# Cross attention of a perceiver: five of seven value units move into their own batch's steps, the opening block is reordered, the context comes in pieces

## The chip, the core and the metric

The program runs on one core of one Trainium2 chip. The metric is the device time of one execution in microseconds (us). TensorE is called PE, VectorE DVE, ScalarE ACT, GpSimd POOL; SP is the engine that here only issues DMA transfers.

## What is computed

Two layers of a perceiver are computed. Each layer has a cross attention over a context, a self attention and a feed-forward part. Only the first part, the cross attention of layer 0, is touched here:

```python
x, ctx_1024            # (16, 64, 256) and (16, 1601, 256), float32
# 16 heads of 16; q from layernorm(x), k and v from the context of the same batch
q = layernorm(x) @ wq + bq
k = ctx_1024 @ wk + bk          # 16 x 1601 x 256
v = ctx_1024 @ wv + bv
p = softmax(q @ k.T * 16 ** -0.5)     # per head
x = x + (p @ v) @ wo + bo
```

The key and value projection of layer 1's cross attention (one shared head of 16) reads the same context and is computed here too ("shared" below), and stored in DRAM for later.

## The kernel before

`cross_attention_block` does the 16 batches one after the other. The work of one batch has two kinds.

**Projection units.** The context of a batch (1602.0 KB, `ctx[b % 2]`, two buffers) is turned into keys and values in 17 units, each a few matmuls of PE into one bank (`project`, L675) and one eviction by DVE (`move_projection`, L702): eight units of keys (two groups of heads, four stretches of columns each), one "shared", seven of values (two tiles of 128 keys each, the last 65 rows), and "turn", which transposes what "shared" gave. POOL splits each unit of keys into a high and a low part (`split_keys`, L643), and counts it in the semaphore `keys_split`.

**Attention steps.** Eight steps n = 0 to 7 for a batch, a pair of heads each. A step has two halves of scores (`score`), two reductions on DVE (`maximum`), two exponentials on ACT (`exps`), and the transposes of the exponentials of the step before (`turn`). Four steps are a group, and `weigh` multiplies a group's probabilities by the values: group 0 of a batch in step 5, group 1 in step 1 of the next batch.

PE runs both kinds in one hand-written order: in each step of batch b it does scores, one unit of batch b+1, transposes, scores, another unit of batch b+1, transposes. Even slots hold keys, odd slots hold "shared" and then the seven values; slot 16 is "turn". The last batch has no units in its steps. Batch 0 has its 17 units in an opening block (`first_block`), which also normalises x, projects the queries (four units, two PSUM banks), stores them in DRAM and loads them back as `q_stack`.

**SP's queue.** SP copies the split keys of batch b+1 into the operand of the scores, `k_stack[n]`, as soon as step n of batch b has been scored, four transfers of 200.2 KB for each n (`stack_keys`). It runs in a fixed order, in which each wait holds back all that stands behind it:

```python
for n in range(PAIRS):
    if n % GROUP_PAIRS == 0:
        sp.wait_ge(keys_split, K_UNITS * (b + 1) + CHUNKS_PER_GROUP * (n // GROUP_PAIRS + 1))
    sp.wait_ge(scored, 2 * (PAIRS * b + n + 1))
    stack_keys(sp, n)
```

At n = 0 it waits for the first four units of keys of batch b+1 (slots 0, 2, 4, 6), and at n = 4 for all eight; the eighth stands in slot 14, in step 7. After n = 7 come the load of the queries of batch b+2, then the context load of batch b+3 (once all units of batch b+1, which read the same buffer, are done), then a store. PE waits for a context at slot 0 (`ctx_loaded` in `project`), just behind the first half of scores of step 0.

A block ends with a barrier of all engines: the next one starts when each engine, SP among them, has come to its end.

Of the kernel before, what the change touches and what calls it, by code (L numbers as in the profile page):

```python
# [21 lines left out]
TILES = TOKENS // P  # L22
# [542 lines left out]
def cross_attention_block(core, layer, x, wo, wk, wv, bk, bv, bo, w_shared, b_shared, scratch, heads_t):  # L565
# [13 lines left out]
    assert U == 2 * PAIRS + 1  # L579

    with ExitStack() as stack:
# [36 lines left out]
        def load_q(sp, b, parity):  # L618
            for copy in range(COPIES):
# [19 lines left out]
        def store_values(sp, b, parity):  # L639
            sp.wait_ge(projection_moved, U * (b + 1))  # L640
            sp.dma_start(core.v1_scratch[b], v_shared[parity][:].rearrange("p t d -> p (t d)")).then_inc(values_stored[parity], 16)

        def split_keys(pool, b, u):  # L643
            g, s, w = k_units[u]
            pool.wait_ge(projection_moved, U * b + units.index(("keys", u)) + 1)
# [8 lines left out]
        def split_shared(pool, b):  # L654
            pool.wait_ge(projection_moved, U * b + units.index(("shared", 0)) + 1)
# [7 lines left out]
        def split_parts(pool, b):  # L663
            for what, i in units:
# [5 lines left out]
        def project(pe, b, parity, u, bank, moved):  # L670

            if u == 0:
                pe.wait_ge(ctx_loaded[parity], 8 * (b - parity) + 16)
            if moved > 0:
                pe.wait_ge(projection_moved, moved)  # L675
            what, n = units[u]
# [25 lines left out]
        def move_projection(dve, b, parity, u, bank):  # L702
            dve.wait_ge(projection_done, U * b + u + 1)
            what, n = units[u]
# [31 lines left out]
        def first_block(first):  # L736
# [11 lines left out]
            EARLY = 3  # L748
# [3 lines left out]
            keys_loaded = core.sem(first, f"{layer}_keys_loaded")  # L752
            values_loaded = core.sem(first, f"{layer}_values_loaded")
# [17 lines left out]
            with core.block() as block:  # L771
                @block.sync
                def _(sp):
                    for i in range(HALVES):
                        half = slice(i * TILES // 2, (i + 1) * TILES // 2)
                        sp.dma_start(x[:, half], dram["x"][:, half]).then_inc(x_loaded[i], 16)
                    sp.dma_start(core.ident[:], dram["ident"]).then_inc(ident_loaded, 16)
                    sp.dma_start(wk[:], dram[f"{layer}_wk"]).then_inc(keys_loaded, 16)
                    sp.dma_start(bk[:], dram[f"{layer}_bk"]).then_inc(keys_loaded, 16)
                    sp.dma_start(w_shared[:], dram["L1_xattn_wkv"]).then_inc(keys_loaded, 16)  # L780
                    sp.dma_start(b_shared[:], dram["L1_xattn_bkv"]).then_inc(keys_loaded, 16)
                    load_ctx(sp, 0, 0)
                    sp.dma_start(wq[:], dram[f"{layer}_wq"]).then_inc(query_loaded, 16)
                    sp.dma_start(bq[:], dram[f"{layer}_bq"]).then_inc(query_loaded, 16)
                    sp.dma_start(wv[:], dram[f"{layer}_wv"]).then_inc(values_loaded, 16)
# [11 lines left out]
                    load_q(sp, 0, 0)  # L797
# [14 lines left out]
                def _(pe):  # L812
                    pe.wait_ge(ident_loaded, 16)
# [8 lines left out]

                    def project_first(u):
                        if u == 0:
                            pe.wait_ge(keys_loaded, 16 * 4)
                            pe.wait_ge(bank_ready, 1)
                        if units[u] == ("values", 0):
                            pe.wait_ge(values_loaded, 16)
                        project(pe, 0, 0, u, banks[:, u % 4], max(u - 3, 0) if units[u][0] != "turn" else u)

                    for u in range(EARLY):
                        project_first(u)
                    pe.wait_ge(query_loaded, 32)
                    for i, (m, half) in enumerate(q_units):
                        pe.wait_ge(x_turned_moved, half + 1)
# [6 lines left out]
                        project_first(EARLY + i)  # L842
# [2206 lines left out]
```

## Time and profile before

| | |
|---|---|
| median of three runs | 2355.4 us (2355.22 to 2358.36) |
| the profiled execution | 2351.33 us, span 2349.1 us |
| PE | busy 92% of the span |
| DVE, ACT, POOL | busy 56%, 42%, 14% |
| granted TensorE clock, mean | 0.959 of full speed |
| context loads (`L_xattn_ctx`) | 16, 1602.0 KB each |

The first attention takes some 890 us of the span. Clocks are shares of TensorE's full speed: 1.0 is its level of 2.4 GHz, 0.5 that of 1.2 GHz. A DMA's time to landing is from its issue to its semaphore.

### The profile page before, as it was taken

The numbers are of one execution on the slowest core, as the hardware profiler recorded it, in microseconds if no ns is written. First come the engines' busy times: TensorE is split into PE (matmuls) and PEld (weight loads), VectorE is DVE, ScalarE is ACT, GpSimd is POOL, SyncE is SP. The second block draws the span as 40 slices with busy tenths as digits, with TensorE's granted clock in tenths as the row PEclk, the third lists the DMA queues.
The fourth block names the chain that finished last, engine by engine and source line by source line (L and its number), as shares of the span: only waits on it lengthen the run. The fifth ranks groups of instructions, "written<-read, shape, count | busy, mean of one in ns | idle before, by whom it ended". The sixth has DMA issues, their size and how long they took to land. (4 is left out here: it accounts for less than half of the span.)

```text
span 2349.1 us, 39843 instructions
## 1 busy us (share of the span) xinstructions
PE 2168.8 (92%) x15922; PEld 1499.2 (64%) x15922; DVE 1315.5 (56%) x2292; ACT 997.3 (42%) x1868; POOL 331.6 (14%) x366
## 2 busy tenths in 40 slices
PE   7999999999999977999998899978999999887796
PEld 4777777777777754555554677854555554545795
DVE  4566666656665634555553344447777772667554
ACT  1555555555555552333433011114666665516121
POOL 3322222232222200000000000014000000000241
PEclk9999999999999978999999899998999999898798
DMA  6877776777777521000000212113111111013312
GB/s 200 197 171 183 179 174 154 173 178 171 183 178 176 127 59 51 6 12 6 6 1 1 115 68 94 55 45 78 28 33 36 24 24 31 23 43 136 135 48 78
DMA packets 101338, 216.18 MB, mean 92 GB/s; under 512 B 58738, under 2 KB 66299, under 8 KB 95428
## 3 DMA queue, kind: packets, MB, share of 16 engines
q1 hardware_dynamic: 98420, 204.93, 35.3%
q0 software_dynamic: 2208, 6.03, 0.8%
q10 hardware_dynamic: 528, 2.69, 0.4%
q8 instruction: 127, 2.08, 0.4%
q14 instruction: 55, 0.45, 0.1%
HBM read 91.16 MB, written 15.20 MB: 45 GB/s over the span
## 5 line engine op out<-in xcount | busy, mean ns | idle before, releaser
L1089 DVE TENSOR_REDUCE L_xattn_maxima<-L_xattn_scores 128x1 f32<-128x1024 f32 (+1 forms) x256 | 253.6, 991 | 239.4 <-PE L_xattn_scores L1012 239.0
L1156 ACT ACTIVATE L_xattn_probs_t<-L_xattn_turned 128x1024 f32<-128x1024 f32 (+1 forms) x256 | 220.8, 862 | 332.6 <-PE L_xattn_turned L1024 332.6
L1997 DVE TENSOR_REDUCE shared_half_maxima<-shared_ring 128x1 f32<-128x578 f32 (+1 forms) x251 | 244.4, 991 | 89.9 <-PE shared_ring L1903 87.1
L2077 ACT ACTIVATE shared_exps<-shared_scores 128x512 f32<-128x512 f32 (+1 forms) x416 | 225.7, 594 | 122.6 <-PE shared_scores L1924 122.0
L1168 ACT ACTIVATE L_xattn_probs<-L_xattn_scores,L_xattn_maxima 128x1024 f32<-128x1024 f32 (+1 forms) x256 | 235.6, 925 | 37.7 <-DVE L_xattn_maxima L1092 37.7
L1024 PEld LDWEIGHTS L_xattn_turned<-ident,L_xattn_probs 128*128 128x128 f32 x1664 | 197.3, 144 | 79.7 <-issue 46.7
L1024 PE MATMUL L_xattn_turned<-ident,L_xattn_probs 128*128 128x128 f32 x1664 | 233.9, 280 | 12.9 <-ACT L_xattn_probs_t L1156 12.0
L686 PE MATMUL L_xattn_projected<-L_xattn_wv,L_xattn_ctx 128*128 128x256 f32 x780 | 193.0, 389 | 0.0
L680 PE MATMUL L_xattn_projected<-L_xattn_ctx,L_xattn_wk 128*128 128x400 f32 x480 | 182.0, 501 | 0.0
L1012 PE MATMUL L_xattn_scores<-L_xattn_k_stack,L_xattn_q_stack 128*128 128x512 f32 (+1 forms) x512 | 159.0, 392 | 22.2 <-ACT L_xattn_probs L1168 11.0
L1924 PE MATMUL shared_scores<-shared_q,shared_k 128*128 128x512 f32 (+1 forms) x416 | 154.1, 449 | 0.1
L686 PEld LDWEIGHTS L_xattn_projected<-L_xattn_wv,L_xattn_ctx 128*128 128x128 f32 x780 | 136.7, 186 | 21.3 <-issue 0.5
L1903 PE MATMUL shared_ring<-shared_k,shared_q 128*128 128x512 f32 x502 | 134.4, 366 | 12.9 <-DMA shared_q<-q_scratch 7.4
L649 POOL CAST L_xattn_k_part<-L_xattn_k_part 128x400 fp32r<-128x400 f32 (+1 forms) x128 | 66.5, 519 | 549.5 <-DVE L_xattn_k_part L710 549.5
L1442 ACT ACTIVATE wide_probs<-wide_scores,wide_stats 128x1024 f32<-128x1024 f32 x64 | 71.4, 1115 | 153.9 <-DVE wide_stats L1392 153.9
L651 POOL TENSOR_TENSOR L_xattn_k_part<-L_xattn_k_part 128x400 fp32r<-128x400 f32 (+1 forms) x128 | 132.8, 1037 | 10.3
L1561 PE MATMUL ffn_merging<-ffn_spread,ffn_task 128*128 128x256 f32 x512 | 129.9, 404 | 4.3 <-DVE ffn_merged L1640 4.3
L1938 PE MATMUL shared_weighed<-shared_exps,shared_v 128*32 128x256 f32 (+1 forms) x1664 | 133.1, 391 | 0.2 <-ACT shared_exps L2077 0.2
L680 PEld LDWEIGHTS L_xattn_projected<-L_xattn_ctx,L_xattn_wk 128*128 128x128 f32 x480 | 91.3, 190 | 46.1 <-issue 0.7
L1325 PE MATMUL wide_scores<-wide_k_t,wide_q_t 128*128 128x512 f32 x256 | 120.5, 593 | 0.0
L1347 PE MATMUL wide_weighed<-wide_probs_t,wide_v 128*128 128x512 f32 x256 | 115.6, 605 | 3.0 <-ACT wide_probs_t L1433 2.3
L1561 PEld LDWEIGHTS ffn_merging<-ffn_spread,ffn_task 128*128 128x128 f32 x512 | 93.2, 197 | 38.0 <-DVE ffn_merged L1640 12.5
(392 smaller groups left out, 3152.7 us busy)
## 6 DMA issues: line engine op xcount, KB each, us to landing
L_xattn_k_stack<-L_xattn_k_part SPq DMA_DIRECT2D x504, 200.2 KB, 4.3
L_xattn_ctx<-in_ctx_t SPq DMA_DIRECT2D x16, 1602.0 KB, 7.0
ffn_task<-in_ffn_task SPq DMA_DIRECT2D x16, 1024.0 KB, 6.7
experts_w_in<-in_expert_in SPq DMA_DIRECT2D x8, 1024.0 KB, 11.5
shared_k<-k_scratch SPq DMA_DIRECT2D x64, 100.1 KB, 3.3
L_xattn_q_stack<-q_scratch SPq DMA_DIRECT2D x128, 32.0 KB, 2.0
k_scratch<-L_xattn_shared_part SPq DMA_DIRECT2D x128, 32.0 KB, 1.7
shared_q<-q_scratch SPq DMA_DIRECT2D x64, 64.0 KB, 3.6
```

The source lines that it names most:

```text
L680: last = nc.tensor.matmul(bank[:, 0:w], wk[:, k, g * P:(g + 1) * P], ctx[parity][:, k, s:s + w], start=k == 0, stop=k == CHUNKS - 1)
L686: last = nc.tensor.matmul(bank[0:rows, i * DIM:(i + 1) * DIM], ctx[parity][:, k, t * P:t * P + rows], wv[:, k, :], start=k == 0, stop=k == ...
L1012: last = nc.tensor.matmul(scores[:, s // BANK, 0:w], q_stack[parity][:, n].rearrange("p h q -> p (h q)"), k_stack[:, n, s:s + w], start=Tr ...
L1024: last = nc.tensor.transpose(turned_tiles[:, i, :], probs[n % 2][:, t * P:(t + 1) * P], core.ident[:])
L1089: nc.vector.reduce_max(maxima[n % 2][:, half:half + 1], cols, axis=AX).then_inc(halves_maxed, 1)
L1156: nc.scalar.activation(probs_t[:, t:t + m, p * P:(p + 1) * P], turned_tiles[:, 0:m, :], ACT.Copy).then_inc(turned_moved, 1)
L1168: nc.scalar.activation(probs[n % 2][:, lo:hi], scores_flat[:, lo:hi], ACT.Exp, bias=maxima[n % 2][:, 2:3], scale=SCALE, accum_out=sums[n / ...
L1561: last = nc.tensor.matmul(merging[:, n % 2, i * 2 * P:(i + 1) * 2 * P], block_of, spread[:].rearrange("p b f -> p (b f)"), start=True, sto ...
L1903: last = nc.tensor.matmul(banks[:, s // BANK - 2 * half, 0:w], q[slot][:, 2 * n:2 * n + 2, :].rearrange("r h q -> r (h q)"), k[slot][:, s: ...
L1924: nc.tensor.matmul(scores[0:m, h, :], k[slot][:, t * P:t * P + m], q[slot][:, h * 8:(h + 1) * 8, :].rearrange("r h q -> r (h q)"), start=T ...
L1997: nc.vector.reduce_max(half_maxima[:, n, half:half + 1], found[:, 0:HALF_STARTS[half + 1] - HALF_STARTS[half]], axis=AX).then_inc(ring_max ...
L2077: nc.scalar.activation(exps[n % 2][0:m, h * BANK:(h + 1) * BANK], scores[0:m, h, :], ACT.Exp, scale=SCALE).then_inc(exps_done, 1)
```

## The change

The units stay the same, and there are as many of them. In each step of batch b the even slots still hold the keys of batch b+1. The odd slots now hold values 2 to 6 of batch b itself (slots 1, 3, 5, 7, 9) and then "shared", values 0 and values 1 of batch b+1 (11, 13, 15). So a batch's context is read until slot 9 of its own steps. The opening block keeps twelve of its seventeen units, and the last batch has five in its steps. The function `order_of` counts a unit's place over all batches, for the waits.

SP loads the context of batch b+2 in batch b, behind `stack_keys` of n = 4, instead of that of batch b+3 at the end of batch b. The store of "shared" moves from behind n = 3 to behind n = 7. In the opening block the first context comes in four pieces of columns, each with its own semaphore; PE does keys 0 ahead of the transposes of x, keys 1 between them, keys 2 between the halves of the queries; and half of the loads of `q_stack` are issued by ACT.

```diff
-    odd_units = [("shared", 0)] + [("values", i) for i in range(V_UNITS)]
-    units = [unit for i in range(K_UNITS) for unit in (("keys", i), odd_units[i])] + [("turn", 0)]
-    U = len(units)
+    first_units = [("keys", i) for i in range(K_UNITS)] + [("shared", 0), ("values", 0), ("values", 1), ("turn", 0)]
+    odd_slots = [(0, ("values", i)) for i in range(2, V_UNITS)] + [(1, ("shared", 0)), (1, ("values", 0)), (1, ("values", 1))]
+    slots = [slot for i in range(K_UNITS) for slot in ((1, ("keys", i)), odd_slots[i])] + [(1, ("turn", 0))]
+    U, FIRST_UNITS = len(slots), len(first_units)
+    def order_of(b, unit):
+        if b == 0 and unit in first_units:
+            return first_units.index(unit)
+        if (0, unit) in slots:
+            return FIRST_UNITS + U * b + (slots if b < BATCH - 1 else last_slots).index((0, unit))
+        return FIRST_UNITS + U * (b - 1) + slots.index((1, unit))
...
-        def project(pe, b, parity, u, bank, moved):
-
-            if u == 0:
-                pe.wait_ge(ctx_loaded[parity], 8 * (b - parity) + 16)
+        def project(pe, b, unit, bank, moved):
+            parity = b % 2
+            what, n = unit
+            if what == "keys" and n == 0 and b > 0:
+                pe.wait_ge(ctx_loaded[parity], 8 * (b + parity))
...
+                    def load_columns(i):
+                        cols = slice(cuts[i], cuts[i + 1])
+                        sp.dma_start(ctx[0][:, :, cols], dram["ctx_t"][0][:, :, cols]).then_inc(columns_loaded[i], 16)
...
-                    load_q(sp, 0, 0)
+                    load_q(sp, 0, 0, range(0, COPIES // 2))
...
+                    act.wait_ge(zeros_ready, 4)
+                    act.wait_ge(query_stored, 16 * 2 * len(q_units))
+                    load_q(act, 0, 0, range(COPIES // 2, COPIES))
                     act.wait_ge(keys_split, CHUNKS_PER_GROUP)
...
                         stack_keys(sp, n)
-                        if n == GROUP_PAIRS - 1:
-                            store_shared(sp, b + 1)
+                        if n == GROUP_PAIRS and ctx_left:
+                            sp.wait_ge(projection_done, order_of(b, ("values", V_UNITS - 1)) + 1)
+                            load_ctx(sp, b + 2, parity)
+                    store_shared(sp, b + 1)
                     if q_left:
                         load_q(sp, b + 2, parity)
-                    if ctx_left:
-                        sp.wait_ge(projection_done, U * (b + 2))
-                        load_ctx(sp, b + 3, 1 - parity)
                     store_values(sp, b + 1, 1 - parity)
...
-                sp.wait_ge(projection_done, U)
-                load_ctx(sp, 2, 0)
                 store_values(sp, 0, 0)
                 for b in range(BATCH - 1):
-                    batch(b, b % 2, b < BATCH - 3, b < BATCH - 2)
+                    batch(b, b % 2, b < BATCH - 2, b < BATCH - 2)
...
+                def fill(b, i, last):
+                    ahead, unit = slots[i]
+                    if ahead == 0 or not last:
+                        project(pe, b + ahead, unit, projected[:, 0], order_of(b + ahead, unit))
```

SP's queue before, at the end of a batch, from `stack_keys` of n = 4 on (`L_xattn_k_stack` is its target, `L_xattn_q_stack` the query load, `L_xattn_ctx` the context load, `v_scratch` the store):

```order
L629 DMA L_xattn_k_stack<-L_xattn_k_part 32x1602 [waits L0_xattn_scored,L0_xattn_keys_split]
L629 DMA L_xattn_k_stack<-L_xattn_k_part 32x1602 x3
L629 DMA L_xattn_k_stack<-L_xattn_k_part 32x1602 [waits L0_xattn_scored]
L629 DMA L_xattn_k_stack<-L_xattn_k_part 32x1602 x3
L629 DMA L_xattn_k_stack<-L_xattn_k_part 32x1602 [waits L0_xattn_scored]
L629 DMA L_xattn_k_stack<-L_xattn_k_part 32x1602 x3
L629 DMA L_xattn_k_stack<-L_xattn_k_part 32x1602 [waits L0_xattn_scored]
L629 DMA L_xattn_k_stack<-L_xattn_k_part 32x1602 x3
L622 DMA L_xattn_q_stack<-q_scratch 16x8x64 x8
L616 DMA L_xattn_ctx<-in_ctx_t 128x3204 [waits L0_xattn_projection_done]
L641 DMA v_scratch<-L_xattn_v_shared 128x208 [waits L0_xattn_projection_moved]
```

The same stretch of SP's queue after the change:

```order
L642 DMA L_xattn_k_stack<-L_xattn_k_part 32x1602 [waits L0_xattn_scored,L0_xattn_keys_split]
L642 DMA L_xattn_k_stack<-L_xattn_k_part 32x1602 x3
L629 DMA L_xattn_ctx<-in_ctx_t 128x3204 [waits L0_xattn_projection_done]
L642 DMA L_xattn_k_stack<-L_xattn_k_part 32x1602 [waits L0_xattn_scored]
L642 DMA L_xattn_k_stack<-L_xattn_k_part 32x1602 x3
L642 DMA L_xattn_k_stack<-L_xattn_k_part 32x1602 [waits L0_xattn_scored]
L642 DMA L_xattn_k_stack<-L_xattn_k_part 32x1602 x3
L642 DMA L_xattn_k_stack<-L_xattn_k_part 32x1602 [waits L0_xattn_scored]
L642 DMA L_xattn_k_stack<-L_xattn_k_part 32x1602 x3
L649 DMA k_scratch<-L_xattn_shared_part 16x512 [waits L0_xattn_shared_split]
L649 DMA k_scratch<-L_xattn_shared_part 16x512 x7
L635 DMA L_xattn_q_stack<-q_scratch 16x8x64 x8
```

The context load has moved up past the copies of n = 5 to 7 and the query load, and stands behind the four copies of n = 4 and their wait for `keys_split`; it now fetches batch b+2 instead of b+3.

PE after the change, from slot 14 of one batch over slots 15 and 16 to slot 0 of the next (the rows of before read the same here, but for the values in slot 15, which were the seventh unit, of 65 rows):

```order
L693 MATMUL L_xattn_projected<-L_xattn_ctx,L_xattn_wk 128x402 [waits L0_xattn_projection_moved]
...
L699 MATMUL L_xattn_projected<-L_xattn_wv,L_xattn_ctx 128x256 [waits L0_xattn_projection_moved]
L699 MATMUL L_xattn_projected<-L_xattn_wv,L_xattn_ctx 128x256 x3
L1052 MATMUL L_xattn_turned<-ident,L_xattn_probs 128x128 [waits L0_xattn_turned_moved,L0_xattn_exps_done]
L1052 MATMUL L_xattn_turned<-ident,L_xattn_probs 128x128 x4
L712 MATMUL L_xattn_projected<-ident,L_xattn_shared_full 128x128 [waits L0_xattn_projection_moved]
L712 MATMUL L_xattn_projected<-ident,L_xattn_shared_full 128x128 x3
L1040 MATMUL L_xattn_scores<-L_xattn_k_stack,L_xattn_q_stack 128x512 [waits L0_xattn_exps_done,L0_xattn_k_stacked0,L0_xattn_q_loaded1]
L1040 MATMUL L_xattn_scores<-L_xattn_k_stack,L_xattn_q_stack 128x512
L693 MATMUL L_xattn_projected<-L_xattn_ctx,L_xattn_wk 128x400 [waits L0_xattn_projection_moved,L0_xattn_ctx_loaded0]
L693 MATMUL L_xattn_projected<-L_xattn_ctx,L_xattn_wk 128x400
```

PE's wait for a context stands where it stood, in slot 0.

## Rows read from the trace of the kernel before

**Rows 1.** The page, busy time; then waits of PE, 200 to 600 us.
```profile
PE 2168.8 (92%) x15922; PEld 1499.2 (64%) x15922; DVE 1315.5 (56%) x2292; ACT 997.3 (42%) x1868; POOL 331.6 (14%) x366
PE L_xattn_scores L1012 <- ACT L_xattn_probs L1168: 2.9, 9, 0.3
```

**Rows 2.** Windows: length, busy of each engine, clock, DMA share, GB/s.
```profile
154.00:205.40 51.40, 50.58 (x467) 38.68 (x465) 31.12 (x57) 28.37 (x49) 14.32 (x19) 1.00 0.75 174
822.50:875.00 52.50, 38.64 (x365) 30.05 (x364) 20.81 (x41) 27.73 (x49) 0.69 (x1) 0.75 0.31 66
```

**Rows 3.** Timeline over the border between two batches: start, length, engine, what.
```profile
152.97 1.04 POOL L651 TENSOR_TENSOR L_xattn_k_part<-L_xattn_k_part 128x402 fp32r<-128x402 f32 x1
154.03 15.23 SPq L629 DMA_DIRECT2D L_xattn_k_stack<-L_xattn_k_part  x16
155.20 0.70 PE L1012 MATMUL L_xattn_scores<-L_xattn_k_stack,L_xattn_q_stack 128*128 128x512 f32 x2 [0.32 <-ACT L_xattn_probs L1168]
155.74 1.50 PE L680 MATMUL L_xattn_projected<-L_xattn_ctx,L_xattn_wk 128*128 128x400 f32 x4
```

**Rows 4.** Timeline of SP's queue, the rest of the same pass.
```profile
169.31 4.20 SPq L622 DMA_DIRECT2D L_xattn_q_stack<-q_scratch  x8
173.55 0.43 SPq L616 DMA_DIRECT2D L_xattn_ctx<-in_ctx_t  x1
```

**Rows 5.** Timeline 154 to 156, and DMA landing of the issue at 155.9 to 156.4.
```profile
154.03 2.57 SPq L629 DMA_DIRECT2D L_xattn_k_stack<-L_xattn_k_part  x4
L_xattn_k_stack<-L_xattn_k_part SPq DMA_DIRECT2D x1, 200.2 KB, 4.0
```

**Rows 6.** Windows of 1 us: key copies start, run; context load runs.
```profile
155.00:156.00 1.00, 0.80 (x3) 0.67 (x4) 0.41 (x3) 1.00 (x4) 0.00 (x0) 1.00 0.97 199
157.00:158.00 1.00, 1.00 (x10) 0.92 (x9) 0.80 (x2) 0.00 (x0) 0.02 (x1) 1.00 1.01 205
176.50:177.50 1.00, 1.00 (x6) 0.65 (x5) 0.87 (x2) 0.00 (x0) 0.00 (x0) 1.00 1.04 410
```

**Rows 7.** Context loads to landing: all sixteen; the second, issued at 6.47.
```profile
DMA to landing us min/median/max: 6.6/7.0/11.1
L_xattn_ctx<-in_ctx_t SPq DMA_DIRECT2D x1, 1602.0 KB, 11.1
```

**Rows 8.** PE's restart after the opening block: timeline, then one window.
```profile
53.25 1.19 PE L1012 MATMUL L_xattn_scores<-L_xattn_k_stack,L_xattn_q_stack 128*128 128x512 f32 x2 [4.03 <-DVE L_xattn_fold L1142]
54.23 2.62 PE L680 MATMUL L_xattn_projected<-L_xattn_ctx,L_xattn_wk 128*128 128x400 f32 x4
53.20:54.20 1.00, 0.95 (x2) 0.83 (x3) 0.00 (x0) 0.00 (x0) 0.00 (x0) 0.50 1.01 199
```

**Rows 9.** Timeline of the opening block's end: queries, their loads, key copies.
```profile
34.31 0.75 DVE L886 SCALAR_TENSOR_TENSOR L_xattn_q_part<-L_xattn_q_psum,L_xattn_bq,L_xattn_q_part 128x512 fp32r<-128x512 f32 x1 [1.75 <-ACT L_xattn_q_part L905]
37.19 5.95 SPq L622 DMA_DIRECT2D L_xattn_q_stack<-q_scratch  x8
37.33 6.83 ACTq L629 DMA_DIRECT2D L_xattn_k_stack<-L_xattn_k_part  x8
43.18 8.26 SPq L629 DMA_DIRECT2D L_xattn_k_stack<-L_xattn_k_part  x8
```

**Rows 10.** Timeline of PE in the last batch: four step starts, two weighings.
```profile
849.90 1.19 PE L1012 MATMUL L_xattn_scores<-L_xattn_k_stack,L_xattn_q_stack 128*128 128x512 f32 x2 [0.40 <-ACT L_xattn_probs L1168]
856.07 1.19 PE L1012 MATMUL L_xattn_scores<-L_xattn_k_stack,L_xattn_q_stack 128*128 128x512 f32 x2 [0.40 <-ACT L_xattn_probs L1168]
866.49 0.70 PE L1012 MATMUL L_xattn_scores<-L_xattn_k_stack,L_xattn_q_stack 128*128 128x512 f32 x2 [0.76 <-ACT L_xattn_probs L1168]
871.57 0.70 PE L1012 MATMUL L_xattn_scores<-L_xattn_k_stack,L_xattn_q_stack 128*128 128x512 f32 x2 [0.76 <-ACT L_xattn_probs L1168]
830.68 3.05 PE L1039 MATMUL L_xattn_weighed<-L_xattn_probs_t,L_xattn_v 128*32 128x128 f32 x104 [0.53 <-ACT L_xattn_probs_t L1156]
857.34 5.31 PE L1039 MATMUL L_xattn_weighed<-L_xattn_probs_t,L_xattn_v 128*32 128x128 f32 x104
```

More of the change, by code:

```diff
@@ L616, in load_ctx, with load_q @@
             sp.dma_start(ctx[parity][:], dram["ctx_t"][ds(b, 1)].rearrange("o p c n -> (o p) c n")).then_inc(ctx_loaded[parity], 16)
-        def load_q(sp, b, parity):
-            for copy in range(COPIES):
+        def load_q(sp, b, parity, copies=range(COPIES)):
+            for copy in copies:
                 for e in range(2):
@@ L654, in split_shared @@
         def split_shared(pool, b):
[L655 removed]
+            pool.wait_ge(projection_moved, order_of(b, ("shared", 0)) + 1)
             if b > 0:
@@ L663, in split_parts @@
         def split_parts(pool, b):
-            for what, i in units:
+            for what, i in first_units if b == 0 else [unit for ahead, unit in slots if ahead == 1]:
                 if what == "keys":
@@ L700, in project, with move_projection @@
             last.then_inc(projection_done, 1)
-        def move_projection(dve, b, parity, u, bank):
-            dve.wait_ge(projection_done, U * b + u + 1)
-            what, n = units[u]
+        def move_projection(dve, b, unit, bank):
+            parity = b % 2
+            what, n = unit
+            dve.wait_ge(projection_done, order_of(b, unit) + 1)
             if what == "keys":
@@ L752, in first_block @@
             keys_loaded = core.sem(first, f"{layer}_keys_loaded")
+            columns_loaded = [core.sem(first, f"{layer}_columns_loaded{i}") for i in range(CHUNKS_PER_GROUP)]
+            shared_loaded = core.sem(first, f"{layer}_shared_loaded")
             values_loaded = core.sem(first, f"{layer}_values_loaded")
@@ L812, in _, with project_first @@
                 def _(pe):
+                    def project_first(u):
+                        what, n = first_units[u]
+                        if what == "keys" and n < CHUNKS_PER_GROUP:
+                            pe.wait_ge(columns_loaded[n], 16)
+                        if what == "shared":
+                            pe.wait_ge(shared_loaded, 32)
+                        if what == "values":
+                            pe.wait_ge(values_loaded, 16)
+                        project(pe, 0, first_units[u], banks[:, u % 4], max(u - 3, 0) if what != "turn" else u)
+                    pe.wait_ge(keys_loaded, 32)
+                    pe.wait_ge(bank_ready, 1)
+                    project_first(0)
                     pe.wait_ge(ident_loaded, 16)
@@ L821, in _ @@
                             last.then_inc(x_turned_ready, 1)
[L823 to L832, printed above, removed]
+                        if t == TILES // 2 - 1:
+                            project_first(1)
                     pe.wait_ge(query_loaded, 32)
                     for i, (m, half) in enumerate(q_units):
+                        if i == CHUNKS:
+                            project_first(2)
                         pe.wait_ge(x_turned_moved, half + 1)
@@ L1053, in batch @@
                         score(b, parity, n, 0)
-                        if not last:
-                            project(pe, b + 1, 1 - parity, 2 * n, projected[:, 0], U * (b + 1) + 2 * n)
+                        fill(b, 2 * n, last)
                         if n == 1 and not first:
@@ L1064, in batch @@
                         score(b, parity, n, 1)
-                        if not last:
-                            project(pe, b + 1, 1 - parity, 2 * n + 1, projected[:, 0], U * (b + 1) + 2 * n + 1)
+                        fill(b, 2 * n + 1, last)
                         if n > 0:
@@ L1070, in batch @@
                             turn(b - 1, PAIRS - 1, 1)
-                        if n == PAIRS - 1 and not last:
-                            project(pe, b + 1, 1 - parity, U - 1, projected[:, 0], U * (b + 1) + U - 1)
+                        if n == PAIRS - 1:
+                            fill(b, U - 1, last)
                 pe.wait_ge(bank_zeroed, 1)
@@ L1119, in keep_heads, with move_slot @@
                                             ALU.add).then_inc(heads_ready, 1)
+                def move_slot(b, i, last):
+                    ahead, unit = slots[i]
+                    if ahead == 0 or not last:
+                        move_projection(dve, b + ahead, unit, projected[:, 0])
                 def batch(b, parity, first, last):
```

49 lines of the change are left out of this document (25 added, 24 removed).

## The prediction

> **What bounds the kernel now.** I read the page first: PE is busy for 92% of the span, no other engine for more than 56% [rows 1]. Then the windows, a batch of the first attention at a time. One batch takes 51.4 us, PE works 50.58 us of them at full clock, and PE's waits in 400 us come to 2.9 us [rows 1, 2]. So in the batches PE is the bound without a gap, and whatever holds PE up is paid in full. The last batch is different: 38.64 us of PE in 52.5, at a mean clock of 0.75 [rows 2]. There the chain of scores, maximum, exponential and transpose sets the pace. The opening block is a third case: PE is done before the block is. SP issues its last key copy at 43.18 + 8.26 = 51.44, and PE's first scores start 1.8 us later, at 53.25 [rows 8, 9]. That end hangs on the queries: they are ready at 35.06, loaded back from 37.19, and only then does SP copy keys.
>
> The view that decides is the timeline over the border of two batches [rows 3]. POOL ends the split of the eighth unit of keys at 154.01, and I call that moment T0. SP, which had waited for it, starts the copies of n = 4 at once, at 154.03. PE starts slot 0 of the next batch, where it waits for a context, at 155.74, which is T0 + 1.73. Before the change the context issued in this pass, at 173.55 [rows 4], is read at the next border, 51.4 us behind this one, at about 207, and lands 6.6 us after its issue at the least, 11.1 at the most [rows 7]; it has over 20 us to spare. PE's wait at slot 0 costs nothing.
>
> **The steady batches: the cost.** Slots keep their number and kind, so PE's work in a batch is the same. What moves is the context load. It now stands behind the copies of n = 4, and these wait for all eight units of keys. The eighth is in slot 14, so SP can't come to the load before T0, however early slot 9 has freed the buffer. The load that goes out behind T0 is the one that PE needs at T0 + 1.73, since batch b loads b+2 and the first step of batch b+1 projects it.
>
> Step by step. SP needs 2.57 us for the four issues [rows 5], so the load is issued at T0 + 2.6. Ahead of it on the DMA engines are 4 x 205 KB. They begin to move at about T0 + 1.0, with the engines fully taken, at 199 to 205 GB/s [rows 6]: 0.82 MB is 3.9 to 4.1 us, to T0 + 4.9. The fourth copy lands 4.0 us after its issue at about T0 + 2.1, hence at T0 + 6.1, so a landing is seen some 1.2 us behind the data. The context, 1.64 MB, moves at up to 410 GB/s alone [rows 6]; with 380 for the whole, 4.3 us, to T0 + 9.2, and with the 1.2 it lands at T0 + 10.4. PE waits from T0 + 1.73: 8.7 us. Bounds: with a landing 6.6 after issue as if nothing were ahead, 7.5 us; with the 11.1 of the one load that had other transfers ahead [rows 7], 12.0 us. I take 8.7.
>
> Everything waits behind PE's slot 0: the transposes of the last exponentials, the second half of scores, thus DVE's maximum and ACT. Nothing of it can be made up, as PE has no slack in the batch. The copies of n = 5 to 7 come some 4 us later, but they are wanted a batch later, in steps 5 to 7.
>
> On top comes the clock. After an idle time of 4.03 us PE restarted at 0.50 [rows 8]: scores in 1.19 instead of 0.70 us, keys in 2.62 instead of 1.50 [rows 3, 8], together 1.6 us lost, and about 0.3 more until it was up. The new idle time is longer, so I take 1.9 a border. Bounds: nothing, and the 5.31 - 3.05 = 2.3 us that a weighing lost at the low level [rows 10].
>
> There are 14 such loads, for batches 2 to 15, and 14 borders. 14 x (8.7 + 1.9) = **+148 us**.
>
> The Trainium skill, "DMA: Bandwidth & Descriptors", section "Queues, rings and completion order", says that each DMA engine takes up descriptors of one ring in order, and that completion is nonetheless not in order. By the first half the context isn't overtaken by the twelve key copies issued behind it, and the sum stays +148; the second half is the opening for the rival "shared engines" below, whose time would be 2551. The rows can't tell, since no context load of before had key copies behind it.
>
> **The opening block: a gain.** Five value units leave, and the queries go ahead of most keys. From the rates above, x, the key weights and the first piece (1.7 MB) should be there at about 8 us (the second context was there at 6.47 + 11.1 = 17.6 with 5.1 MB moved [rows 7]). Two units of keys and sixteen transposes then stand ahead of the queries, with a unit of keys between their halves; at some 3 us for a unit while the clock is low and 1.7 us for a query unit, the last query unit leaves PE at about 25 and its low part is ready at 27, where it was 35.06 [rows 9]. So the loads of `q_stack` start at 29 instead of 37.19, and two queues take half of 5.95 each: 32. Then 16 key copies, 3.28 MB. If the engines limit them (205 GB/s, rows 6), 16 us, the last issued about 4 us before it lands: 44. If only the issuing queues do, 8.3 us [rows 9]: 40. PE with its twelve units would be done before either. Against 51.44 that is a gain of 7 to 11; the engines were fully taken in rows 6, so I take **-7 us** (bounds -4, if the queries slip, and -11).
>
> The Trainium skill, in the same page's section "Issuing engines are not separate DMA queues", says that DMAs of several issuing engines run on the same sixteen DMA engines and interleave. By that the second queue saves issue time only, and the opening gives 7; by the durations on the issuing queues alone it would give 11.
>
> **The last batch: five units more.** They fall into steps 0 to 4. A step took 6.17 us at the low clock (849.90 to 856.07) and 5.08 at full clock (866.49 to 871.57) [rows 10]. A value unit is some 1.7 us of PE, of which the step's idle time covers most; I put the step at 5.4. If the fill keeps the clock up, three steps gain 0.75 each and the weighing 2.3, against two steps that lose 0.3: about **-4 us**, of which I take -3.5 since the clock may fall later instead. Bounds: -6, and +4 if the clock falls all the same and the units run at half speed.
>
> Sum: 148 - 7 - 3.5 = +138. The profiled execution took 2351.33 (span 2349.1), so 2489; the runs' median lies 4 above the profiled time. I write 2491, between the two, here and for the rivals.
>
> **Rivals.**
> - *The load is cheap.* It lands 6.6 after issue and the clock stays up: 14 x 7.5 = 105, less 10.5: +94, 2448. For it: every load of mid-attention landed in about 7 us. Against it: none of them had a 200 GB/s stream ahead.
> - *Shared engines.* The twelve key copies behind the load share the engines with it, and the landing goes to the 11.1 row or beyond: 14 x (12.0 + 2.3) = 200, less 10.5: +190, 2543. At an even share, 8.6 us instead of 4.3 after T0 + 4.9, it lands at T0 + 14.7; 13.0 of wait and 1.9 for the clock give 2551. Against it: the issues come in one queue.
> - *No wait (the other side).* SP gets to the load early enough to hide it, and only opening and last batch count: -10.5, 2343. It decides when the wait at slot 0 is under 10.5 / 14 = 0.75 us, so the load has to be issued 5 us before T0. For it: the buffer is free from slot 9, some 20 us before. Against it: the order rows show the `keys_split` wait ahead of it, and rows 3 show SP released by the eighth split, 0.02 us behind it.
> - *The opening gives far more.* Even 20 us there would leave +125.
>
> **How the numbers follow.** My forecast has 0.78, the cheap load 0.07, shared engines 0.10, no wait 0.04, some 0.01 for anything near zero. The forecast's own spread is 7.5 to 9.7 for the wait, 1.3 to 2.3 for the clock, 14 times, plus 5 either way for the ends: 2465 to 2515. The range takes half of the cases next to it: 2453 to 2530. Runs of one kernel agree to about 0.2%, 4.7 us, which is what can be told from no change. Faster has 0.04, same 0.01, slower 0.95.
>
> **What the profile after would show.** Right: SP's context load 2.6 us behind the end of POOL's eighth split, landing 7 to 9 us after issue; PE idle some 9 us ahead of keys in slot 0, released by the DMA of the context, 14 times; windows at clock 0.5 behind each; batches of about 62 us; first scores at 42 to 49 us; PE busy for some 88% of the span. Wrong: a wait of under 1 us there (no wait), landings of 11 us and more (shared engines), full clock behind the idle time (the 1.9), steps at clock 0.5 in the last batch (the -3.5). What would upset all of it is another engine's wait in the steady steps which I don't see, or a second wait of PE in the batch, such as for `k_stack` of steps 5 to 7.

## The result

The changed kernel takes 2530.45 us (median of four runs, 2529.76 to 2531.08), the kernel before 2356.88 (2355.22 to 2360.24). The ratio is 1.0734, with a 95% interval of 1.0716 to 1.0753. The forecast was 2491 us, slower, with a range of 2453 to 2530; the direction and the mechanism came as told, and the size was 39 us short: the time lies at the range's upper end, 0.45 us above it.

The page of the changed kernel. In the second row, one of the page's groups, the part behind the last bar is PE's idle time just ahead of the keys units, and what ended it:

```profile
PE 2202.9 (87%) x15922; PEld 1515.4 (60%) x15922; DVE 1314.1 (52%) x2292; ACT 997.5 (39%) x1868; POOL 331.3 (13%) x366
L693 PE MATMUL L_xattn_projected<-L_xattn_ctx,L_xattn_wk 128*128 128x400 f32 x480 | 202.4, 548 | 140.5 <-DMA L_xattn_ctx<-in_ctx_t 140.5
```

PE has the same 15922 matmuls as in [rows 1], and 140.5 us of wait for a transfer that it never waited for before. The waits of PE from 80 to 900 us, and then the landing of all whole context loads, from the view of their line:

```profile
PE L_xattn_projected L693 <- DMA L_xattn_ctx<-in_ctx_t: 130.9, 13, 12.3
DMA to landing us min/median/max: 8.7/9.6/12.0
```

Thirteen waits lie in that stretch and fourteen in the program, each about 10 us. The landing of 6.6/7.0/11.1 [rows 7] has become 8.7/9.6/12.0.

The timeline over one border of batches, the counterpart of [rows 3]:

```profile
221.11 1.04 POOL L664 TENSOR_TENSOR L_xattn_k_part<-L_xattn_k_part 128x402 fp32r<-128x402 f32 x1
222.18 2.63 SPq L642 DMA_DIRECT2D L_xattn_k_stack<-L_xattn_k_part  x4
223.93 0.71 PE L1040 MATMUL L_xattn_scores<-L_xattn_k_stack,L_xattn_q_stack 128*128 128x512 f32 x2
224.85 0.97 SPq L629 DMA_DIRECT2D L_xattn_ctx<-in_ctx_t  x1
234.38 3.04 PE L693 MATMUL L_xattn_projected<-L_xattn_ctx,L_xattn_wk 128*128 128x400 f32 x4 [9.74 <-DMA L_xattn_ctx<-in_ctx_t]
237.21 1.91 PE L1052 MATMUL L_xattn_turned<-ident,L_xattn_probs 128*128 128x128 f32 x8
238.77 0.83 PE L1040 MATMUL L_xattn_scores<-L_xattn_k_stack,L_xattn_q_stack 128*128 128x512 f32 x2
239.41 2.25 PE L699 MATMUL L_xattn_projected<-L_xattn_wv,L_xattn_ctx 128*128 128x256 f32 x8
241.50 0.71 PE L1052 MATMUL L_xattn_turned<-ident,L_xattn_probs 128*128 128x128 f32 x5
```

T0 is 222.15. SP starts the four copies 0.03 us behind it and the context load at T0 + 2.70, and PE gets its keys going at T0 + 12.2. Behind the wait four pieces are slow: keys 3.04 for 1.50, transposes 1.91 for 1.04, scores 0.83 for 0.51, values 2.25 for 1.97. Added up that is 3.0 us, but part of it overlaps or falls into waits that were there before; what it adds to a batch is worked out further down. Two windows behind the restart, then six from the time of the load, in the form of [rows 6]:

```profile
234.30:235.30 1.00, 0.92 (x2) 0.59 (x3) 0.00 (x0) 0.00 (x0) 0.00 (x0) 0.50 0.92 205
238.30:239.30 1.00, 1.00 (x5) 0.95 (x4) 0.00 (x0) 0.14 (x1) 0.92 (x2) 0.50 1.08 237
...
226.10:227.10 1.00, 0.00 (x0) 0.00 (x0) 0.00 (x0) 0.00 (x0) 0.00 (x0) 0.61 0.97 192
229.10:230.10 1.00, 0.00 (x0) 0.00 (x0) 0.00 (x0) 0.00 (x0) 0.00 (x0) 0.50 1.09 384
230.10:231.10 1.00, 0.00 (x0) 0.00 (x0) 0.00 (x0) 0.00 (x0) 0.00 (x0) 0.50 0.99 295
231.10:232.10 1.00, 0.00 (x0) 0.00 (x0) 0.00 (x0) 0.00 (x0) 0.00 (x0) 0.50 0.84 252
232.10:233.10 1.00, 0.00 (x0) 0.00 (x0) 0.00 (x0) 0.00 (x0) 0.00 (x0) 0.50 1.14 327
233.10:234.10 1.00, 0.00 (x0) 0.00 (x0) 0.00 (x0) 0.00 (x0) 0.00 (x0) 0.50 0.78 147
```

The clock is at its lower level for five microseconds behind this restart; over the fourteen it is 3.0 to 5.8 us, by windows of 0.1 us. The load's traffic starts at about T0 + 5, as told, reaches 384 GB/s, and then runs at 252 to 327 and ends at 147, which is not the pace of a context load alone (410 in [rows 6]).

Cut at the first scores of each batch, the spans of the two profiled executions (2349.1 and 2529.1 us) compare so:

| part | before | after | difference | forecast |
|---|---|---|---|---|
| opening, to the first scores | 53.25 | 40.51 | -12.7 | -7, with batch 0 |
| batch 0 | 50.52 | 55.71 | +5.2 | |
| batches 1 to 14, sum | 720.6 | 909.0 | +188.4 | +148 |
| last batch, to the output projection | 67.06 | 62.43 | -4.6 | -3.5 |
| the rest of the program | 1457.7 | 1461.4 | +3.8 | 0 |

In the mean a batch grew from 51.47 to 64.93 us, by 13.46.

### The profile page after: what moved, and what is told of

Its sections match the earlier page's. It is cut to its first block and busy times, and to the rows that moved or that the text cites. A ratio compares the mean times of both kernels' runs of the same rounds, so it can differ in the third digit from the quotient of the medians.

```text
span 2529.1 us, 39851 instructions
## 1 busy us (share of the span) xinstructions
PE 2202.9 (87%) x15922; PEld 1515.4 (60%) x15922; DVE 1314.1 (52%) x2292; ACT 997.5 (39%) x1868; POOL 331.3 (13%) x366
## 5 line engine op out<-in xcount | busy, mean ns | idle before, releaser
L693 PE MATMUL L_xattn_projected<-L_xattn_ctx,L_xattn_wk 128*128 128x400 f32 x480 | 202.4, 548 | 140.5 <-DMA L_xattn_ctx<-in_ctx_t 140.5
L1052 PEld LDWEIGHTS L_xattn_turned<-ident,L_xattn_probs 128*128 128x128 f32 x1664 | 204.6, 148 | 83.0 <-issue 52.7
L1202 ACT ACTIVATE L_xattn_probs<-L_xattn_scores,L_xattn_maxima 128x1024 f32<-128x1024 f32 (+1 forms) x256 | 235.6, 925 | 38.5 <-DVE L_xattn_maxima L1123 38.5
L1052 PE MATMUL L_xattn_turned<-ident,L_xattn_probs 128*128 128x128 f32 x1664 | 240.6, 285 | 10.1 <-ACT L_xattn_probs_t L1190 7.8
L699 PE MATMUL L_xattn_projected<-L_xattn_wv,L_xattn_ctx 128*128 128x256 f32 x816 | 204.8, 393 | 6.4 <-DVE L_xattn_k_part L724 6.4
L724 DVE TENSOR_SCALAR L_xattn_k_part<-L_xattn_projected,L_xattn_bk 128x400 f32<-128x400 f32 x120 | 76.1, 634 | 184.6 <-PE L_xattn_projected L693 166.2
L699 PEld LDWEIGHTS L_xattn_projected<-L_xattn_wv,L_xattn_ctx 128*128 128x128 f32 x816 | 145.4, 189 | 29.5 <-DVE L_xattn_k_part L724 6.7
L1937 PE MATMUL shared_ring<-shared_k,shared_q 128*128 128x512 f32 x502 | 135.3, 368 | 12.3 <-DMA shared_q<-q_scratch 7.7
## 6 DMA issues: line engine op xcount, KB each, us to landing
L_xattn_k_stack<-L_xattn_k_part SPq DMA_DIRECT2D x504, 200.2 KB, 4.5
L_xattn_ctx<-in_ctx_t SPq DMA_DIRECT2D x15, 1602.0 KB, 9.6
experts_w_out<-in_expert_out SPq DMA_DIRECT2D x8, 512.0 KB, 12.7
```

The costliest lines, as they stand in the source:

```text
L693: last = nc.tensor.matmul(bank[:, 0:w], wk[:, k, g * P:(g + 1) * P], ctx[parity][:, k, s:s + w], start=k == 0, stop=k == CHUNKS - 1)
L699: last = nc.tensor.matmul(bank[0:rows, i * DIM:(i + 1) * DIM], ctx[parity][:, k, t * P:t * P + rows], wv[:, k, :], start=k == 0, stop=k == ...
L1052: last = nc.tensor.transpose(turned_tiles[:, i, :], probs[n % 2][:, t * P:(t + 1) * P], core.ident[:])
L1202: nc.scalar.activation(probs[n % 2][:, lo:hi], scores_flat[:, lo:hi], ACT.Exp, bias=maxima[n % 2][:, 2:3], scale=SCALE, accum_out=sums[n / ...
L1937: last = nc.tensor.matmul(banks[:, s // BANK - 2 * half, 0:w], q[slot][:, 2 * n:2 * n + 2, :].rearrange("r h q -> r (h q)"), k[slot][:, s: ...
```

## The experiments

The times in brackets are those of the kernel before on the same chip. A single run stands beside medians where no ratio is given. "Batch" is one of batches 1 to 14, cut as above.

### The load ahead of the wait

```diff
 for n in range(PAIRS):
+    if n == GROUP_PAIRS and ctx_left:
+        sp.wait_ge(projection_done, order_of(b, ("values", V_UNITS - 1)) + 1)
+        load_ctx(sp, b + 2, parity)
     if n % GROUP_PAIRS == 0:
         sp.wait_ge(keys_split, K_UNITS * (b + 1) + CHUNKS_PER_GROUP * (n // GROUP_PAIRS + 1))
     sp.wait_ge(scored, 2 * (PAIRS * b + n + 1))
     stack_keys(sp, n)
-    if n == GROUP_PAIRS and ctx_left:
-        sp.wait_ge(projection_done, order_of(b, ("values", V_UNITS - 1)) + 1)
-        load_ctx(sp, b + 2, parity)
```

> The changed kernel with one edit: in SP's loop the context load stands ahead of the wait for keys_split at n = 4, so it goes out once slot 9 has freed the buffer. Theory (the load's place behind that wait is the whole loss): the 14 borders lose their 13.8 us each (193.6 us between the first scores and the last batch in the two traces), so 2530.5 - 193.6 = 2337 us, no wait of PE for the context, faster than before by some 20 us. Rival (the new split of units or the shared DMA engines cost something of their own in a batch): the wait goes, but batches stay longer than 51.4 us and the time stays above 2357.

It took 2361.37 us (2356.8), ratio 1.0018, interval 1.0006 to 1.003. All waits for the context are gone; SP's queue now reads:

```profile
121.90 14.43 SPq L642 DMA_DIRECT2D L_xattn_k_stack<-L_xattn_k_part  x16
136.37 0.97 SPq L629 DMA_DIRECT2D L_xattn_ctx<-in_ctx_t  x1
147.61 14.56 SPq L642 DMA_DIRECT2D L_xattn_k_stack<-L_xattn_k_part  x16
```

The load goes out 11 us ahead of the eighth split. So 169 of the 174 us hang on the place of one issue in one queue. But the rival had a part too: eight of the fourteen batches take 52.4 us and not 51.4 (five of the others, up to 56.02, hold pauses that are told at the end), and the kernel isn't faster than before. The timeline of PE shows where, first around slot 9, then at slots 15 and 16:

```profile
178.15 0.51 PE L1040 MATMUL L_xattn_scores<-L_xattn_k_stack,L_xattn_q_stack 128*128 128x512 f32 x2
178.50 1.05 PE L699 MATMUL L_xattn_projected<-L_xattn_wv,L_xattn_ctx 128*65 128x256 f32 x4
179.60 0.74 PE L1052 MATMUL L_xattn_turned<-ident,L_xattn_probs 128*128 128x128 f32 x5
181.09 0.70 PE L1040 MATMUL L_xattn_scores<-L_xattn_k_stack,L_xattn_q_stack 128*128 128x512 f32 x2 [0.75 <-ACT L_xattn_probs L1202]
...
198.24 0.52 PE L1040 MATMUL L_xattn_scores<-L_xattn_k_stack,L_xattn_q_stack 128*128 128x512 f32 x2
198.59 1.97 PE L699 MATMUL L_xattn_projected<-L_xattn_wv,L_xattn_ctx 128*128 128x256 f32 x8
200.40 0.71 PE L1052 MATMUL L_xattn_turned<-ident,L_xattn_probs 128*128 128x128 f32 x5
201.35 0.66 PE L712 MATMUL L_xattn_projected<-ident,L_xattn_shared_full 128*128 128x128 f32 x4 [0.24 <-DVE L_xattn_v L731]
201.76 0.72 PE L1040 MATMUL L_xattn_scores<-L_xattn_k_stack,L_xattn_q_stack 128*128 128x512 f32 x2
```

The half step with the short value unit lasts 2.94 us (178.15 to 181.09), no less than one with a full unit, as PE then waits for ACT. Before the change the short unit stood in slot 15, and "turn" filled that wait. Now slot 15 is full and "turn" comes on top: 3.52 us from 198.24 to 201.76, 0.57 more than before. The half step behind it, with the keys of slot 0, takes 3.08 instead of 2.68 in the median of the batches: its keys wait until DVE has emptied the bank that "turn" has just filled. Together that is the 1.0 us.

### The short unit back in slot 15

On top of the edit above, one line. It renames units: the one of 65 rows becomes value unit 1.

```diff
     v_units = [list(range(t, min(t + 2, KEY_TILES))) for t in range(0, KEY_TILES, 2)]
+    v_units.insert(1, v_units.pop())
```

> The kernel with the early context load, with one edit more: the short value unit (65 rows, 1.05 us) becomes unit 1, so it stands in slot 15 ahead of the transposes of slot 16, where it stood before the change, instead of in slot 9. Theory (the batches of 52.4 us with the early load, against 51.4 before, come from the short unit: in slot 9 the step can't get shorter than its chain through ACT, PE waits 0.75 us, and slots 15 and 16 are full): batches go back to 51.4, 2361.4 - 15 = 2346 us, faster than before by 10 to 12. Rival (the 1.0 us comes from the context load or from the other exchanges of units): 2361 stays.

2342.96 us (2359.21), ratio 0.9931, interval 0.9919 to 0.9944. Ten of the fourteen batches take 51.4 to 51.5 us. So the exchange of a full for a short unit was worth 1.0 us a batch, and this kernel beats both. Of the 19 us between the fourteen batches of the two kernels (743.2 and 724.0 us in the profiled executions) it makes some 13; the rest is fewer pauses.

### The load ahead of the four copies

```diff
     if n % GROUP_PAIRS == 0:
         sp.wait_ge(keys_split, ...)
+    if n == GROUP_PAIRS and ctx_left:
+        sp.wait_ge(projection_done, ...)
+        load_ctx(sp, b + 2, parity)
     sp.wait_ge(scored, 2 * (PAIRS * b + n + 1))
     stack_keys(sp, n)
```

> The changed kernel with one edit: the context load stands behind the wait for keys_split of n = 4, but ahead of the four key copies of n = 4; it goes out at T0 instead of T0 + 2.7, with nothing ahead and sixteen copies behind it. Theory (only what stands ahead counts): it lands 7 us after issue, T0 + 7; a border costs 13.8 - 5.2 = 8.6, so 2530 - 73 = 2457. Rival (the copies issued behind it share the engines): it still takes 9.6 to land, T0 + 9.6; a border costs 11.2, so 2530 - 36 = 2494.

2484.78 us, between the two expectations. PE's fourteen waits and the landing:

```profile
  PE L_xattn_projected L693: 87.1, 14
DMA to landing us min/median/max: 7.8/8.5/11.7
```

With the load at T0 PE waits 6.2 us. Nothing is ahead of the load, and it still takes 8.5 us instead of 7.0: the copies behind it cost some 1.5.

### The copies behind held back

```diff
         load_ctx(sp, b + 2, parity)
+        sp.wait_ge(ctx_loaded[parity], 8 * (b + 2 + parity))
```

> The changed kernel with one edit: SP, behind the context load, waits until it has landed before it issues the key copies of n = 5. The four copies ahead of it stay. Theory (followers share the engines with the load, which is why it lands 9.6 us after issue and not 7.8): the landing comes down to 7.5 to 8, a border by 1.6 to 2, so 2530 - 25 = 2505. Rival (the four copies ahead are all that delays it): landing stays at 9.6 and the time at 2530.

2501.43 us, as the theory had it.

```profile
  PE L_xattn_projected L693: 116.4, 14
DMA to landing us min/median/max: 7.3/7.9/9.3
```

The landing comes down from 9.6 to 7.9, and the wait from 10.0 to 8.3 a border. The four copies ahead are all still there. My sum had the landing at 7.8 after issue: it is right for a load with four copies ahead and none behind.

### PE kept busy during the wait

```diff
             if what == "keys" and n == 0 and b > 0:
+                if b > 1:
+                    for i in range(72):
+                        nc.tensor.transpose(bank[:, 0:P], core.ident[:], core.ident[:])
                 pe.wait_ge(ctx_loaded[parity], 8 * (b + parity))
```

(PE's wait for the free bank is moved ahead of these lines.)

> The changed kernel with one edit: at slot 0 of the 14 borders PE does 72 transposes of the identity into the free projection bank ahead of its wait for the context (results are overwritten; 9.4 us at 0.13 each), so PE has work while it waits. Theory (3.0 of the 13.8 us of a border are the low clock after the idle time: keys 3.04 instead of 1.50, transposes 1.91 instead of 1.03, scores, values): the clock stays at 1.00, a border costs 10.8, so 2530 - 42 = 2488. Rival (the clock falls anyway, or the transposes outlast the wait): 2530 or more.

2516.51 us: 14 us less, not 42. The transposes took 0.11 us each and ended before the load had landed:

```profile
222.06 8.09 PE L691 MATMUL L_xattn_projected<-ident 128*128 128x128 f32 x72
232.96 3.04 PE L696 MATMUL L_xattn_projected<-L_xattn_ctx,L_xattn_wk 128*128 128x400 f32 x4 [2.81 <-DMA L_xattn_ctx<-in_ctx_t]
235.79 1.24 PE L1055 MATMUL L_xattn_turned<-ident,L_xattn_probs 128*128 128x128 f32 x8
```

An idle time of 2.81 us was enough for slow keys here, though the transposes behind them were less slow. It wasn't always: five of the fourteen borders restarted at 0.50, behind 2.34 to 4.46 us of idle time, and nine at 1.00, behind 0.71 to 2.70. So the same with 100:

> As the changed kernel with transposes ahead of PE's wait for the context, with 100 of them instead of 72 (11.2 us, longer than the wait). With 72 PE was idle for 2.8 us behind them and did the keys at the low clock again, 3.04 us. Theory (the clock falls for an idle PE, and 3.0 us of a border's 13.5 are its price): keys take 1.50 behind the transposes, the borders of 64.9 us come to 61.9 to 62.5, so 2530 - 38 = 2492 or a little less. Rival (the low clock has to do with the transfers, or with the batch's start): 2.4 to 3.0 us for the keys.

```profile
225.12 11.13 PE L691 MATMUL L_xattn_projected<-ident 128*128 128x128 f32 x100
236.10 1.51 PE L696 MATMUL L_xattn_projected<-L_xattn_ctx,L_xattn_wk 128*128 128x400 f32 x4
237.44 1.04 PE L1055 MATMUL L_xattn_turned<-ident,L_xattn_probs 128*128 128x128 f32 x8
```

Keys take 1.51, so the slow restart was the clock's and not the transfers'. The time was 2515.44, not 2492. The transposes outlast the landing: most batches came to 63.2 to 63.3 us, more than the 62.5 that I had named as their upper end. At this border SP issued the load at 225.35 and it landed 9.6 us later, 1.1 us ahead of the keys; over the fourteen the keys start 0.88 us behind the landing in the mean, against 0.04 in the changed kernel. What the clock was worth shows behind the wait, from the start of the keys to the second half of scores, and in the half step after it: 4.23 and 3.12 us in the changed kernel, 2.15 and 2.94 here, 2.14 and 2.94 in the kernel before (means of the fourteen). That is 2.3 us a border, and not the 3.0 that I had put.

### One queue for the loads of q_stack

On top of the kernel with the short unit in slot 15:

```diff
-                    load_q(sp, 0, 0, range(0, COPIES // 2))
+                    load_q(sp, 0, 0)
...
-                    act.wait_ge(zeros_ready, 4)
-                    act.wait_ge(query_stored, 16 * 2 * len(q_units))
-                    load_q(act, 0, 0, range(COPIES // 2, COPIES))
```

> The kernel with the early load and the short unit last, with one edit: all eight loads of q_stack are issued by SP again, none by ACT. Theory (the sixteen key copies of the opening are limited by the DMA engines, and what the opening gains in issue time is given back in batch 0, where DVE waits for their landing): first scores come up to 2 us later, but first scores plus batch 0 end within 1 us of the run beside it, and so does the time. Rival (the second queue is a good part of the opening's 12.7 us): the end of batch 0 comes 3 us later or more.

2343.67 us, beside 2342.96. First scores come at 43.29 instead of 39.60, and batch 0 takes 50.76 instead of 55.70: it ends at 94.1 instead of 95.3. The second queue brings its first scores earlier and nothing at the end of batch 0. Why is in the changed kernel's opening: timeline, then the landing of the sixteen key copies by queue.

```profile
28.11 1.75 SPq L635 DMA_DIRECT2D L_xattn_q_stack<-q_scratch  x4
29.90 8.38 SPq L642 DMA_DIRECT2D L_xattn_k_stack<-L_xattn_k_part  x8
29.96 8.54 ACTq L642 DMA_DIRECT2D L_xattn_k_stack<-L_xattn_k_part  x8
40.51 0.70 PE L1040 MATMUL L_xattn_scores<-L_xattn_k_stack,L_xattn_q_stack 128*128 128x512 f32 x2 [2.38 <-DMA L_xattn_k_stack<-L_xattn_k_part]
48.56 0.63 DVE L724 TENSOR_SCALAR L_xattn_k_part<-L_xattn_projected,L_xattn_bk 128x400 f32<-128x400 f32 x1 [6.08 <-DMA L_xattn_k_stack<-L_xattn_k_part]
49.24 3.46 PE L699 MATMUL L_xattn_projected<-L_xattn_wv,L_xattn_ctx 128*128 128x256 f32 x8 [6.43 <-DVE L_xattn_k_part L724]
...
L_xattn_k_stack<-L_xattn_k_part SPq DMA_DIRECT2D x8, 200.2 KB, 8.2
L_xattn_k_stack<-L_xattn_k_part ACTq DMA_DIRECT2D x8, 200.2 KB, 8.9
```

Both queues issue eight copies in 8.4 to 8.5 us, but the copies land 8 to 9 us after issue in the median, not 4.3: the issue ends by 38.5 and the last copy lands at 48.4. DVE must not overwrite `k_part` for batch 1 before they have been read from it, waits 6.08 us, and PE waits 6.43 behind it.

### The last batch of the kernel before, filled

```diff
                             project(pe, b + 1, 1 - parity, 2 * n + 1, projected[:, 0], U * (b + 1) + 2 * n + 1)
+                        if last and n < 5:
+                            pe.wait_ge(projection_moved, U * BATCH)
+                            for i in range(15):
+                                nc.tensor.transpose(projected[:, 0, 0:P], core.ident[:], core.ident[:])
```

> The kernel before with one edit: in steps 0 to 4 of the last batch, where no unit stands, PE does 15 transposes of the identity (1.7 us) into the free projection bank in the odd slot. Their results are never read. Theory (the last batch gained 4.6 us with five units more because they keep the clock up): the last batch falls from 67.1 us to the 62.4 that it takes after the change, 2356.8 - 4.6 = 2352. Rival (it gained since its weights or its start were better): no change, or longer by the 1.5 us of the fill.

2353.61 us (2359.21), ratio 0.9981, interval 0.9968 to 0.9994. The last batch took 61.55 us, against 67.06 before and 62.43 after the change, and transposes that nothing reads did it: the clock makes the gain, not the kind of work.

### The end of the last batch filled too

On top of the short unit in slot 15, 15 transposes in each odd slot of steps 5 to 7, and 12, 8 and 4 ahead of the last two turns and the last weighing:

```diff
+                    elif i > 10 and i % 2:
+                        keep_busy(15)
```

> The kernel with the early load and the short unit last, with one edit: in steps 5 to 7 of the last batch, and ahead of the last two turns and the last weighing, PE does 4 to 15 transposes of the identity into the free projection bank; nothing reads them. Theory (an only partly busy PE falls to the low clock there, as in steps 6 and 7 and the last weighing of the changed kernel: steps of 6.17 us, weighing 5.8 instead of 3.05): the last batch goes from 61.8 to some 57 us, 2343 - 5 = 2338. Rival (the transposes stand in the way of the chain through ACT, or the clock falls all the same): 2343 or more.

2339.74 us (2358.66), ratio 0.9935, interval 0.9914 to 0.9956. The end of the last batch, first with the short unit in slot 15, then with the filled end; the clock is the third number from the right:

```profile
850.00:881.00 31.00, 20.51 (x258) 16.64 (x247) 7.99 (x19) 12.36 (x20) 0.00 (x0) 0.72 0.00 1
```

```profile
846.00:877.00 31.00, 26.22 (x373) 23.10 (x372) 11.03 (x26) 15.26 (x26) 0.00 (x0) 1.00 0.01 2
```

The last batch went from 61.82 to 56.59 us in the profiled executions. The intervals of the two ratios overlap, so the whole program doesn't prove the 5 us.

## Why the prediction came out as it did

**The bound, T0 and the order in SP's queue** were right in each number: load issued 2.70 behind T0 (2.6 told), fourteen waits, everything else behind PE. The rival "no wait" fell, and the first experiment shows that one issue moved past one wait takes the loss away.

The fourteen batches grew by 188.4 us, 40 more than the 148 told. The traces give it by stretches (means of the fourteen, us; "scores" are the two matmuls at the head of each half step):

| stretch | before | after | more | told |
|---|---|---|---|---|
| first scores of step 0 to the keys of slot 0 | 0.54 | 10.75 | 10.21 | 8.7 |
| keys of slot 0 to the second scores | 2.14 | 4.23 | 2.09 | 1.9, with the next |
| second scores of step 0 to step 1 | 2.94 | 3.12 | 0.18 | |
| slots 15 and 16 | 2.95 | 3.52 | 0.57 | 0 |
| the rest of the batch | 42.90 | 43.31 | 0.41 | 0 |
| batch | 51.47 | 64.93 | 13.46 | 10.6 |

**The landing was mis-sized, and that is the largest part: 14 x (10.21 - 8.7) = 21 us.** "With 380 for the whole, 4.3 us, to T0 + 9.2, and with the 1.2 it lands at T0 + 10.4": it was T0 + 12.2 at the border shown, and 9.6 after issue as the median, where 7.8 was told. I let the twelve copies behind the load cost nothing in the forecast and gave them a case of their own, at an even share. The truth lies between: held back, they give 7.9; in place, 9.6.

**The clock was nearly right**, 2.3 for 1.9 a border: 5 us. I took the loss from a restart behind 4.03 us of idle time, where the clock was up again after some 3 us; behind waits of 9.2 to 12.3 us it was at 0.50 for 3.0 to 5.8, and not longest behind the longest wait.

**"Slots keep their number and kind, so PE's work in a batch is the same" was a step that didn't hold.** PE's work is the same, its time isn't: a short unit is worth something only where the work next to it fills the wait for ACT. With the early load that costs 1.0 us a batch. In the changed kernel only the 0.57 of slots 15 and 16 shows, 8 us in batches 1 to 14; the other 0.4 would fall into the half step where PE waits for the context anyway. The order rows showed the 65-row unit in another slot, and I had written that down without costing it.

**The rest of the batch** gives 6 us, of which three pauses of 1.34, 1.52 and 1.74 us make 4.6; they are told at the end. 21 + 5 + 8 + 6 = 40.

One working in the spread was off as well: 14 x (7.5 + 1.3), less the ends and another 5, gives 2461 and not 2465 for its lower end. The range doesn't depend on it.

**The opening: -7 told, 12.7 - 5.2 = 7.5 measured**, by a way that I had only half. The 205 GB/s of the engines does limit the sixteen copies. But it didn't hold back the issues, as I had assumed; it moved the landing out, past the end of the block, into a wait of DVE in batch 0. The last of the sixteen lands at 48.4, against 55.4 before, 7.0 earlier. The Trainium skill's sentence ("DMA: Bandwidth & Descriptors", "Issuing engines are not separate DMA queues") that DMAs of all issuing engines run on the same engines and interleave bears out here: with one queue for the loads of `q_stack` batch 0 ends at 94.1, with two at 95.3.

**The last batch: -3.5 told, -4.6 measured**, by the clock, as told, which the experiment with the filled last batch shows; a step with a value unit took 5.09 us (1022.93 to 1028.02), where 5.4 was put.

**The rest of the program**, +3.8 us, was told as nothing. About 0.7 of it are there when the shared attention starts, and most lies between 1937 and 2182 us of the kernel before, where the granted clock is 0.88 after and 0.91 before (2000 to 2150). The program is the same there, and over the eleven profiled executions this part took 1456.4 to 1462.8 us, 1456.5 with the early load. So the 3.8 us are no more than what such executions differ by; why the clock falls otherwise is open.

## What to carry to other kernels

A load moved up in a queue gets no earlier than the slowest wait still ahead of it: look for the wait, not for the place. A prefetch whose buffer is read longer loses its slack, and the first thing to check is when the queue that issues it gets there. When units of unequal length change places, cost the short one by what fills its neighbour; and where PE waits for its partners at the end of a stage, work that nobody reads can hold the clock.

## What the runs showed beyond that

- A DMA queue's issue time says little about the engines behind it. In the opening eight copies of 200.2 KB were issued in 8.4 us by one queue beside another that did the same, with landings of 8.2 and 8.9 us instead of 4.7 to 5.0 when the queues took turns.
- A load of 1602.0 KB landed in 7.0 us alone, in 7.9 with four copies of 200.2 KB ahead, in 8.5 with sixteen behind, in 9.6 with four ahead and twelve behind. So copies issued later delay an earlier load in the same queue, but by less than an even share would (12.1 after issue, by the prediction's rival). The Trainium skill ("DMA: Bandwidth & Descriptors", "Queues, rings and completion order") says that each DMA engine takes up descriptors of one ring in order. I had leaned on that; no run here contradicts it, but order of start doesn't keep the followers' cost out.
- Behind 2.34 to 4.46 us of idle time PE restarted at the low level five times, and behind 0.71 to 2.70 at the high one nine times. Transposes of the identity that nothing reads, 0.11 us each, held the high one through a wait of some 10 us.
- PE paused now and then inside a run of matmuls with nothing to wait for in the profile, 0.8 to 2.68 us long, one to six times in the fourteen batches of every other kernel here and not once above 0.8 in those of the kernel before. The order of units isn't the reason: the kernel before with its last batch filled has three, up to 1.71 us, in batches that the edit doesn't touch. One of them:

```profile
451.08 0.53 PE L1067 MATMUL L_xattn_weighed<-L_xattn_probs_t,L_xattn_v 128*32 128x128 f32 x12 [1.79 <-issue]
```

That row is of the kernel with the early load, whose longest batch (56.02 us) holds a pause of 1.73 us with the clock at 0.50 behind it. The kernel with the short unit in slot 15 had two such pauses, and its two longest batches (52.92 and 53.28 us) are theirs. What they are wasn't tried, but the traces point somewhere: all 31 pauses of 0.8 us and more end 2.3 to 3.1 us behind the start of a transfer on queue 8, which the page lists as "instruction". These transfers of 16 KB come 14 to 18 us apart in the mean, one for some 250 of PE's matmuls and weight loads in the kernel before. So PE may have waited for its own instructions; that isn't shown.
